# Batch 0's residual-side tiles, the stack cast, the second stack transfer and the last chunk's hidden buffers in a Macaron transformer layer

## The reference, cut to what matters

```
x = x + 0.5 * ffn(layernorm(x))
x = x + attn(layernorm(x))          # attn(h) = h + gate * out, so the normed input is added too
x = x + 0.5 * ffn(layernorm(x))

ffn(x):  h = silu(x @ wg.T) * (x @ wu.T);  return h @ wd.T        # hidden 384, int weights / 127
attn(h): r = rmsnorm(h) * norm_w
         q, k, v = r @ Wq, r @ Wk, r @ Wv                         # 4 query heads, 2 key heads, 32 wide
         q, k = l2norm(q), l2norm(k)
         p = softmax(causal(q @ k.T * exp(log_temperature)))
         return h + gate * ((p @ v) @ Wo)
```

## Time and profile before

| what | value |
|---|---|
| median of three runs | 430.47 us (430.47 to 430.57) |
| the profiled execution's own time | 430.8 us |
| its span in the trace | 429.0 us |
| TensorE busy | 393.1 us (92% of the span) |
| ScalarE busy | 370.0 us (86%) |
| VectorE busy | 349.1 us (81%) |
| GpSimd busy | 299.7 us (70%) |
| granted TensorE clock | 0.999 of full |

### The profile page before, as it was taken

One profiled execution on the slowest core, in us unless ns is written; L12 is line 12 of the kernel. 1 busy time (PEld: TensorE's weight loads), 2 busy tenths in 40 slices (PEclk: granted clock), 3 DMA queues, 4 the chain that ended last, 5 costly groups with the idle time before them and its releaser, 6 DMA issues.

```text
span 429.0 us, 13351 instructions
## 1 busy us (share of the span) xinstructions
PE 393.1 (92%) x5403; PEld 219.8 (51%) x5403; DVE 349.1 (81%) x887; ACT 370.0 (86%) x497; POOL 299.7 (70%) x381
## 2 busy tenths in 40 slices
PE   0689999898898899999999999999999999999994
PEld 0346666574444434635546446456354346765754
DVE  4889999689596997997998979968769848878554
ACT  4799999776797698999998998999987989999950
POOL 5689999985799858857758578581123658999850
PEclk9999999999999999999999999999999999999999
DMA  6487523513605706418237148055142225566532
GB/s 171 102 194 156 67 49 50 99 27 76 124 2 76 125 2 127 74 16 143 46 75 101 26 76 128 2 107 93 20 87 46 39 38 75 111 136 100 126 96 79
DMA packets 119233, 35.25 MB, mean 82 GB/s; under 512 B 101632, under 2 KB 119168, under 8 KB 119168
## 3 DMA queue, kind: packets, MB, share of 16 engines
q1 hardware_dynamic: 117888, 34.02, 43.1%
q10 hardware_dynamic: 1280, 0.33, 0.3%
HBM read 4.98 MB, written 4.19 MB: 21 GB/s over the span
## 4 chain that ended last, share of the span: by engine, by line
PE 55%; DVE 13%; ACT 10%; DMA 8%; issue 6%; POOL 6%; SPq 1%; DVEq 0%; ACTq 0%
PE ps L740 11%; PE ps L770 10%; PE ps L777 10%; PE ps L511 9%; DMA QKT<-ST 5%; ACT XN L463 3%; PE ps L804 3%; PE ps L575 3%; PE ps L564 3%; DVE H L332 3%; ACT PT L884 3%; PE ps L600 3%; DVE RD L245 2%; PE ps L747 2%; DMA XT<-w_int 2%
## 5 line engine op out<-in xcount | busy, mean ns | idle before, releaser
L884 ACT ACTIVATE PT<-ps,k_exp 128x1024 f32<-128x1024 f32 x144 | 153.9, 1122 | 14.1 <-PE ps L747 8.0
L511 PE MATMUL ps<-XT,WT 128*128 128x512 f16 x384 | 93.9, 383 | 6.2 <-DVE H L332 2.0
L740 PE MATMUL ps<-QKT 128*32 128x512 f16 (+1 forms) x1280 | 86.6, 359 | 5.0 <-DMA QKT<-ST 3.3
L770 PE MATMUL ps<-PT,V 128*32 128x512 f32 (+3 forms) x768 | 76.1, 486 | 0.0
L777 PE MATMUL ps<-PT,ones 128*32 128x512 f32 (+3 forms) x768 | 76.1, 486 | 0.0
L438 POOL TENSOR_TENSOR HL<-H,HH 128x1024 f16<-128x1024 f32 x31 | 66.6, 2148 | 8.3 <-ACT HH L487 5.3
L332 DVE SCALAR_TENSOR_TENSOR H<-SG,k_isilu,ps 128x1536 f32<-128x1536 f32 x32 | 57.9, 1808 | 13.9 <-ACT SG L481 6.3
L511 PEld LDWEIGHTS ps<-XT,WT 128*128 128x128 f16 x384 | 34.5, 98 | 50.6 <-issue 10.5
L463 ACT ACTIVATE XN<-X,NB,RS 128x128 f32<-128x128 f32 x128 | 52.5, 483 | 2.5 <-POOL NB L410 2.5
L481 ACT ACTIVATE SG<-ps,k_silu 128x1536 f32<-128x1536 f32 x32 | 48.8, 1526 | 4.4 <-DVE H L332 4.3
L740 PEld LDWEIGHTS ps<-QKT 128*32 128x32 f16 x1280 | 31.0, 96 | 41.2 <-issue 16.0
(11 more groups left out here) (140 smaller groups left out, 664.3 us busy)
## 6 DMA issues: line engine op xcount, KB each, us to landing
result<-X SPq DMA_DIRECT2D x15, 256.0 KB, 2.5
X<-in_L_attn_x SPq DMA_DIRECT2D x7, 512.0 KB, 4.6
X<-in_L_attn_x SPq DMA_DIRECT2D x2, 256.0 KB, 4.7
XT<-w_int SPq DMA_TRANSPOSE x32, 3.1
QKT<-ST SPq DMA_TRANSPOSE x18, 5.8
AXT<-AS SPq DMA_TRANSPOSE x16, 3.0
w_int<-in_L_ffn_w_gate SPq DMA_DIRECT2D x1, 192.0 KB, 4.0
w_int<-in_L_ffn_w_up SPq DMA_DIRECT2D x1, 192.0 KB, 4.7
```

Of the source, the lines that this page charges most:

```text
L511: i = e.matmul(out[:, j, :], WT[:, wp, w * NJ + j, :], XT[k % 2][:, xp, :], start=a == 0, stop=a == len(passes) - 1)
L740: i_ = e.matmul(dst[r, :].rearrange("p (s a n) -> p s a n", a=2, n=P), QKT[k % 2][:, i // TPC, NH + hp, key0 + r.start:key0 + r.stop], q.r ...
L770: e.matmul(sums_of(h, 0, n), V[k % 2][:, i, v0:v0 + HD], weights_of(g, h, o, n), start=i == 0, stop=i >= TPC * qc, skip_group_check=True)
L884: e.activation(dst, SCORES[(SLOT0[g] + i) % 2][:, :, :], ACT.Exp, scale=k_exp[:, 0:1]).then_inc(a_exp, 1)
```

## The change

Four edits.

1. On GpSimd the four `add_norm` calls of batch 0 (blocks 2, 3, 4, 5; sixteen tensor_scalar instructions) go away. VectorE gets them in its batch 0: blocks 2 and 3 after the statistics of blocks 4 and 5; block 4 after the statistics of blocks 6 and 7; block 5 at the batch's end, after `wo_out`. In the same place `stack_hi2` of block 3 goes behind the statistics of blocks 6 and 7 and behind `add_norm` of block 4, where it stood ahead of both. In later batches GpSimd keeps `add_norm`; in batches 1 to 4 `stack_hi2(m0 + 1)` stands between the statistics of the two blocks, where it stood ahead of both. Each `add_norm` from block 1 on waits for the count of those before it.
2. From batch 1 on ScalarE's `stack_hi(m0, 0)` comes at group 3, and the copy `v_out` of the second half's second part at group 4; they were the other way round.
3. The stack of block 1 goes as three transfers: query heads 0 and 1, query heads 2 and 3, then the keys. TensorE waits for the first two at group 3 and for the keys at group 7.
4. Chunk 15 of feed-forward 2 has its hidden values, high and low parts in the memory of attention's `PT`, and `hidden` no longer waits for the down projection there.

```diff
@@ -131,6 +131,10 @@
         QKT = [sb(f"QKT{i}", [P, QCS, NQK, CH], f16) for i in range(2)]
         V = [sb(f"V{i}", [P, TPB, NQKV]) for i in range(2)]
         PT = [sb(f"PT{i}", [P, 2, 2 * CH]) for i in range(2)]
+        PT_words = [v.rearrange("p a n -> p (a n)") for v in PT]
+        H_LAST = PT_words[0][:, 0:NJ * CH].rearrange("p (j n) -> p j n", n=CH)
+        HH_LAST = PT_words[0][:, NJ * CH:2 * 2 * CH].bitcast(f16)
+        HL_LAST = PT_words[1][:, 0:CH].bitcast(f16)
         PVS = sb("PVS", [P, 2, CH])
         RD = sb("RD", [P, CH])
         MX = sb("MX", [P, 2, TPC, NH])
@@ -171,7 +175,7 @@
             "full", "free", "cp", "s", "exp", "pv", "pvc", "rd", "on", "oh", "ol", "mx", "last")]
         s_half, s_hl_last = sem("s_half"), sem("s_hl_last")
         a_xh0, a_fac = sem("a_xh0"), sem("a_fac")
-        d_k0, d_q0 = sem("d_k0"), sem("d_q0")
+        d_k0, d_q0, d_q1, d_q2 = sem("d_k0"), sem("d_q0"), sem("d_q1"), sem("d_q2")
         d_f, d_x, d_t, d_u = [[sem(f"{n}{i}") for i in range(2)] for n in ("d_f", "d_x", "d_t", "d_u")]
 
         w16 = WT[:, :, :, :].rearrange("p s j n -> p (s j) n")
@@ -296,9 +300,13 @@
                 if lo <= c < hi:
                     e.wait_ge(s_xin[i], 16)
 
-        def hidden_16(k):
-
-            return H[k % 2].rearrange("p j n -> p (j n)")[:, CUT:]
+        def hidden_parts(ph, k):
+
+            return (H_LAST, HH_LAST, HL_LAST) if ph and k == NC - 1 else (H[k % 2], HH[k % 2], HL[k % 2])
+
+        def hidden_16(ph, k):
+
+            return hidden_parts(ph, k)[0].rearrange("p j n -> p (j n)")[:, CUT:]
 
         def ffn_dve(e, ph, only=None, after={}, between={}):
             def stats(k, c):
@@ -327,9 +335,9 @@
                 g = c + NC * ph
                 e.wait_ge(s_silu, g + 1)
                 e.wait_ge(s_up, g + 1)
-                if k >= 2 or ph:
+                if (k >= 2 or ph) and not (ph and k == NC - 1):
                     e.wait_ge(s_dn, g - 1)
-                e.scalar_tensor_tensor(H[k % 2][:, :, :], SG[:, :, :], k_isilu[:, 0:1], U,
+                e.scalar_tensor_tensor(hidden_parts(ph, k)[0][:, :, :], SG[:, :, :], k_isilu[:, 0:1], U,
                                        ALU.mult, ALU.mult).then_inc(s_h, 1)
 
             def residual(k, c):
@@ -356,14 +364,14 @@
 
                 if ph and k in (0, NC - 2):
                     e.wait_ge(s_h, c + NC * ph + 1)
-                    e.tensor_copy(HH[k % 2][:, :], hidden_16(k)).then_inc(s_hh, 1)
+                    e.tensor_copy(hidden_parts(ph, k)[1][:, :], hidden_16(ph, k)).then_inc(s_hh, 1)
 
             def last_h_lo(k, c):
 
                 if ph and k == NC - 1:
                     residual_of(c - 2, DN)
                     e.wait_ge(s_hh, c + NC * ph + 1)
-                    e.tensor_tensor(HL[k % 2][:, :], hidden_16(k), HH[k % 2][:, :], ALU.subtract)\
+                    e.tensor_tensor(hidden_parts(ph, k)[2][:, :], hidden_16(ph, k), hidden_parts(ph, k)[1][:, :], ALU.subtract)\
                         .then_inc(s_hl_last, 1)
                     residual_of(c - 1, XP.rearrange("p (t d) -> p t d", t=TPC))
 
@@ -484,7 +492,7 @@
                 if ph and k in (0, NC - 2):
                     return
                 e.wait_ge(s_h, c + NC * ph + 1)
-                e.activation(HH[k % 2][:, :], hidden_16(k), ACT.Copy).then_inc(s_hh, 1)
+                e.activation(hidden_parts(ph, k)[1][:, :], hidden_16(ph, k), ACT.Copy).then_inc(s_hh, 1)
 
             def amid(k, c):
 
@@ -561,7 +569,7 @@
                 full = [(t, j) for j in range(NW) for t in range(TPC) if j * CH + t * P < CUT]
                 split = [(t, j) for j in range(NJ) for t in range(TPC) if j * CH + t * P >= CUT]
                 for n, (t, j) in enumerate(full):
-                    e.matmul(dn[:, t, :], H[k % 2][:, j, t * P:(t + 1) * P], WD[:, j, :],
+                    e.matmul(dn[:, t, :], hidden_parts(ph, k)[0][:, j, t * P:(t + 1) * P], WD[:, j, :],
                              start=n == 0, stop=False, skip_group_check=True)
                 for hp, wp in [(0, 0), (0, 1)][:1 + low] + [(1, 0)]:
                     if hp and ph and k == NC - 1:
@@ -572,7 +580,7 @@
                         e.wait_ge(s_hh, g + 1)
                     for t, j in split:
                         o = j * CH + t * P - CUT
-                        i = e.matmul(dn[:, t, :], (HH, HL)[hp][k % 2][:, o:o + P],
+                        i = e.matmul(dn[:, t, :], hidden_parts(ph, k)[1 + hp][:, o:o + P],
                                      WT[:, wp, 2 * NJ + j, :], start=False, stop=hp == 1,
                                      skip_group_check=True)
                 i.then_inc(s_dn, 1)
@@ -706,6 +714,8 @@
             else:
                 e.wait_ge(a_coef, 5 * m - 5)
             e.wait_ge(a_xn, m + 1)
+            if m:
+                e.wait_ge(a_y, m)
             for t in range(TPC):
                 i = e.tensor_scalar(tile(c, t), tile(c, t), A1[q][:, t:t + 1], B1[q][:, t:t + 1],
                                     ALU.mult, ALU.subtract)
@@ -726,6 +736,10 @@
                         e.wait_ge(d_q0, 16)
                     else:
                         e.wait_ge(d_t[0], 16)
+                elif g == G0 and isinstance(b, int) and b == 0 and not shift:
+                    e.wait_ge(d_q2 if hp else d_q1, 16)
+                elif g == NG - 3 and isinstance(b, int) and b == 0 and not shift:
+                    e.wait_ge(d_t[1], 16)
                 elif hp == 0 and tiles_[0][0] == 0:
                     e.wait_ge((d_u if shift else d_t)[qc], b * 16 + 16)
                 for i, o, n in tiles_:
@@ -960,11 +974,11 @@
                             x_hi(2 + g, g)
                         if g == (2 if k == 0 else 0):
                             qkv_out(k + 1, m0, k, b, 0)
-                        for c, at in enumerate((3, 3) if k == 0 else (1, 3)):
+                        if g == (4 if k == 0 else 3):
+                            stack_hi(m0, 0)
+                        for c, at in enumerate((3, 3) if k == 0 else (1, 4)):
                             if g == at:
                                 v_out(k + 1, m0 + 1, k, b, 1, c)
-                        if g == 4:
-                            stack_hi(m0, 0)
                         if g == 5:
                             squares(k + 1, m0 + 1, k, b, 1)
                         if g == (9 if k == 0 else 8):
@@ -1034,9 +1048,6 @@
                 if later:
                     rstds(m0 + 2, q)
                     rstds(m0 + 3, q + 1)
-                if k == 0:
-                    add_norm(e, 2, 2, 2)
-                    add_norm(e, 3, 3, 3)
                 if k >= 1:
                     o_lo(e, b * 2 - 1)
                 if k >= 1 and later:
@@ -1046,9 +1057,7 @@
                                     ("x_hi", 1), ("x_lo", 1)])
                 if nxt:
                     stack_lo(m0, 0)
-                if k == 0:
-                    add_norm(e, m0 + 2, m0 + 2, q)
-                if later:
+                if k >= 1 and later:
                     add_norm(e, m0 + 3, m0 + 3, q + 1)
                 o_lo(e, b * 2)
                 if later:
@@ -1227,6 +1236,8 @@
                 if k == 0:
                     stats(m0 + 2, m0 + 2, q)
                     stats(m0 + 3, m0 + 3, q + 1)
+                    for m in range(2, 4):
+                        add_norm(e, m, m, m)
                 if k >= 1:
                     o_norm(e, b * 2 - 1)
                 if not nxt:
@@ -1253,15 +1264,22 @@
                     unit(k + 1, 20 * b + 40, m0 + 1, 1)
                 if nxt:
                     rows(m0, k, b, 0)
-                    stack_hi2(m0 + 1, 1)
                 if k + 3 < B:
                     stats(m0 + 4, m0 + 4, 2 - q)
+                    if k == 0:
+                        stats(m0 + 5, m0 + 5, 3 - q)
+                        add_norm(e, m0 + 2, m0 + 2, q)
+                if nxt:
+                    stack_hi2(m0 + 1, 1)
+                if 1 <= k < B - 3:
                     stats(m0 + 5, m0 + 5, 3 - q)
                 if not nxt:
                     ffn_dve(e, 1, [("moments", c) for c in range(4, NE)])
                 if nxt:
                     wo_out(k, b, ("wo", 0), b * 2)
                     rows(m0 + 1, k, b, 1)
+                if k == 0:
+                    add_norm(e, m0 + 3, m0 + 3, q + 1)
             drive(e, step, B, 1, 3, not shift)
             last_pv_out(e)
             wo_out(B - 1, B - 1, ("wo", 0), 2 * B - 2)
@@ -1312,6 +1330,11 @@
                     stack(0, NH, NQK, d_k0)
                     stack(0, 0, 2, d_q0)
                     stack(0, 2, NH, d_t[0])
+                    return
+                if m == 1 and not shift:
+                    stack(1, 0, 2, d_q1)
+                    stack(1, 2, NH, d_q2)
+                    stack(1, NH, NQK, d_t[1])
                     return
                 stack(m, 0, NQK, d_t[m % 2])
                 if shift:
```

## The result

The changed kernel takes 427.75 us (median of 8 runs, 426.95 to 429.25), the kernel before beside it 430.52 us (8 runs, 430.39 to 430.9): ratio 0.9937, 95% interval 0.9925 to 0.995. It is 2.8 us faster where 5.4 were forecast, and 0.15 us past the range. The runs are spread more widely than before, and they part by the granted clock: five at 1.0 took 426.95 to 428.07 us (median 427.29), three at 0.996 took 428.38 to 429.25 us. The profiled execution is one of the latter: 429.13 us, span 427.3 us. Even the five are 2.2 us slower than forecast, so the clock is not the whole of the miss.

The account below looks back on a forecast made before the run. TensorE was taken to bound the kernel, with slack only in batches 0 and 1 and at the end. Gains of 1.1 + 1.1 + 0.9 + 1.0 + 0 + 1.3 = 5.4 us off 430.47 gave 425.1 us, range 423.6 to 427.6.

Parts of the forecast that it names:

- `add_norm` of blocks 2 and 3: Batch 0: VectorE does these in its 5.10 us hole, block 2's stack lands sooner; gain 1.1 us, bounds 0 and 1.11.
- `add_norm` of blocks 4 and 5: Batches 0 to 1: OL and AXT waits go, a 2 us wait for block 3's stack arises; gain 0.9 us.
- rest of batch 1: Group 3 of batch 1 to batch 2: block 4's stack wait goes, ScalarE catches up; gain 1.0 us, bounds 0 and 1.3.
- own buffers: Chunk 15 at the end: hidden(15) starts 1.8 us sooner; gain 1.3 us, bounds 0.9 and 1.8.
- Second stack in pieces: Batch 0, group 3: three pieces of block 1's stack remove TensorE's 1.12 us wait; gain 1.1 us, bounds 0.3 and 1.12.
- Steady batches: Later batches: ScalarE's sooner cast does not wait for QN; gain 0, bounds 0.2 us a batch either way.
- Rival D: Group 3 of batches 1 to 6: the sooner cast stalls ScalarE waiting for QN; 431.4 us, slower, chance 0.03.
- C: Everything lines up: block 3's stack wait is 1 us, steady batches give 0.2 us each; 423.4 us, chance 0.08.
- B: Batch 0: pieces pay their cost in series, third piece and AXT land 4 us late; 428.6 us, chance 0.08.
- The prediction's own sign of being wrong: ScalarE idle for QN, first AXT holding TensorE over 1 us, or batch 0's gain not still there at batch 2's group 0.
- Rival A: Batches 0 and 1: the stack of block 3 or 4 lands as late as 7.5 us; 427.1 us, chance 0.18.

Follow-up runs that it names:

- the copy first: The changed kernel with VectorE's `stack_hi2(3)` moved ahead of `add_norm(4)`, nothing else: 426.15 us, ratio 0.9889 to the kernel before.
- the kept-busy kernel: The changed kernel with twelve unused 512-column matmuls on TensorE ahead of group 3 of batch 1: 427.33 us, ratio 0.9918 to the kernel before.
- the moved tiles alone: The kernel before with only `add_norm` of blocks 2 to 5 on VectorE and block 3's second copy behind statistics: 431.9 us, ratio 1.0016.
- the late issue: The changed kernel with `stack_hi2(3)` ahead of `add_norm(4)`, but block 3's stack issued only after `add_norm(4)`: 429.16 us, ratio 0.9956 to the kernel before.

## Why the prediction was wrong, step by step

The terms of the sum, with what TensorE's scores and the span show against the one trace of before (us gained; the two profiled executions of the changed kernel, the second taken beside the later runs):

| term | forecast | 429.13 us | 428.27 us |
|---|---|---|---|
| pieces, and `add_norm` of blocks 2 and 3 | 2.2 | 1.6 | 1.8 |
| `add_norm` of blocks 4 and 5 | 0.9 | -0.6 | -0.6 |
| rest of batch 1 | 1.0 | -0.1 | -0.1 |
| from batch 2 to the last chunk | 0 | -0.8 | 0.0 |
| own buffers | 1.3 | 1.6 | 1.4 |
| sum | 5.4 | 1.7 | 2.5 |

**What held.**

- *Own buffers:* 1.3 us forecast, 1.4 us to the last residuals in the trace, 1.6 alone.
- *Second stack in pieces:* the 1.12 us wait became 0.21, and that is for the second piece. The first piece landed 4.6 us after its issue, not 3.2, the three held the queue 4.7 us, not 3.7, and the AXT cost 0.7 us, not 0.4. Worth 0.7 us alone and about 1 with the copy first.
- *`add_norm` of blocks 2 and 3:* in the hole with 1.79 us to spare, the stack of block 2 issued at 125.64 where 125.7 was forecast. It landed after 7.2 us instead of the 6.3 seen before, which left 0.41 us of the wait.
- *Steady batches:* 29.66 us a batch in nearly every trace from batch 4 on (batch 3 took up to 0.3 more), and no stall for QN.

Rival D is out, and C, since the wait was 2.8 us and not 1. B is out too: the third piece landed 3.3 us after its own issue. The 2.0 us behind B is what "DMA: Bandwidth & Descriptors" of the Trainium skill (Anatomy of one DMA) gives for transfers that GpSimd issues; these are SyncE's, and no run here shows that cost paid in series.

**The step that failed is "`add_norm` of blocks 4 and 5"**, and with it the next. The new wait at group 3 of batch 1 was forecast, and as a transfer for the stack of block 3. Its size was wrong, for two reasons.

First, VectorE was late with what stands ahead of the copy. "`unit(3)` ends near 132.5" was 134.09 (133.13 + 0.96), because two root steps took 1.09 and 1.08 us where before they had taken 0.32 and 0.18. GpSimd, freed of its tiles, now did its AS low parts beside them, at 130.55. Then `add_norm(4)` took 2.31 us, not 1.5, with GpSimd's `stack_lo(3)` at 136.65 beside it; `add_norm(5)` took 1.10. This delayed the copy and the issue to 139.32, against 138.1 to 138.7. `stack_lo(3)` itself ended at 138.57, so of these delays some 0.75 us reached the issue, which is what the copy first gave back. The exposure had been written down, from the page "GPSIMD Engine Reference" of the Trainium skill and the 1.39 against 0.69 us, and then not counted. That the two engines' instructions slow each other is read from rows that stand side by side. The two long root steps are in all ten traces in which VectorE has the tiles and in none of the four in which GpSimd has them; `add_norm(4)` takes 2.3 to 2.4 us where it meets `stack_lo(3)` first and 1.5 where the copy does. No experiment isolates it.

Second, I gave the transfer 5.8 to 6.4 us; it took 7.2. So the scores came at 146.63 instead of 144.5, and 0.96 us were left of 3.1. (The lower bound of -0.6, from a 7.5 us transfer issued at 138.7, is nearer -0.8 by its own numbers.)

**"Rest of batch 1"** had ScalarE "caught up by the new wait", 1.0 us gained. But a wait of 2.8 us on TensorE is not neutral: in the profiled executions of the changed kernel the clock went to half behind it, which cost 1.5 us. That is shown by the kept-busy kernel, and by the moved tiles alone, where the same wait left the clock full. At full clock the stretch took 19.4 us in both, 1.4 less than before, so without the clock this term would have come. When the clock falls behind such a wait and when it doesn't stays open. The largest idle time of TensorE's matmuls in this stretch had been 1.12 us before, and the granted clock over it was 1.00, so no row could have priced it; but a new gap larger than any in the trace should have had a bound of its own. The profiled execution lost another 0.7 us at group 3 of batch 2, where a stack landed after 8.6 us; the second profile of the same kernel has 6.1 us there and no wait.

The prediction's own sign of being wrong came: the gain of batch 0, 1.6 us, was down to 0.85 at group 0 of batch 2.

Rival A, transfers taking the gain back, was the case that came: 427.1 us at 0.18, built on a 7.5 us landing. It had nothing on the clock, so that the median is within 0.7 us of it is partly luck. It deserved the larger chance: in the trace before, five of the fifteen six-head transfers took 7.0 us or more, and a landing that must be early enough twice is not a 60% case.

## What to carry over

When buffers come free sooner, the next transfer's landing is the new bound: price it from the spread of its landings, not the median, and count what stands between its last operand and its issue, since the whole gain hangs on that one place. Put the operation that releases a transfer ahead of any work that only must be done some time: here one call moved by one place gave 2.5 us, as much as the four edits together. Of that the sooner issue itself is 0.75 to 1.0 us; the rest came with a transfer that also took 1.7 us less, for a reason that stays open, and with a clock that stayed full. When work leaves one of VectorE and GpSimd, look at what now falls beside the other's instructions. A gap on TensorE that is longer than any before can cost again afterwards through the clock, so look at the granted clock of the stretch behind it, and try the change with the gap filled before judging its parts.

## What the runs showed of the hardware

A six-head stack transfer's landing is not its packets' end. In the changed kernel the packets of block 3's stack end by 144.5 us and it lands at 146.5; with the copy first they end by 144.0 us and it lands at 143.84. Windows (width, PEclk, DMA share, GB/s), changed kernel, then copy first:

```profile
144.00:144.50 0.50, 1.00 0.58 121
144.50:145.00 0.50, 1.00 0.00 0
145.00:146.00 1.00, 1.00 0.00 0
```

```profile
143.00:143.50 0.50, 1.00 0.48 89
143.50:144.00 0.50, 1.00 0.12 33
144.00:145.00 1.00, 1.00 0.00 0
```

The two values repeat. Where VectorE has the tiles, this transfer took 7.1 or 7.2 us in five profiled executions that issued it 6.3 to 6.5 us after the scores of batch 1 began, and 5.5 us in three that issued it 5.6 us after. Where GpSimd has them it took 5.5 to 5.8 us in four, issued 5.9 to 7.2 us after. So the moment alone does not decide, and what does stays open. The stack of block 2 lands 7.2 us after its issue in the copy-first trace too. Since the copy first and the late issue differ in this landing, their 3 us are the effect of the issue together with it. Pieces of two heads landed 3.2 to 5.3 us after their issue.
